# Attention result turned on the vector engine and moved by 64-byte transfers, in a fused attention and mixture-of-experts kernel

## The reference

```python
# attention: H = 8 heads, dqk = 2, dv = 16
q = (x @ Wq.T + bq).reshape(B, M, H, dqk)
k = (x @ Wk.T + bk).reshape(B, M, H, dqk)
v = (x @ Wv.T + bv).reshape(B, M, H, dv)
scores = einsum('bmhd,bnhd->bhmn', q, k) / sqrt(dqk)
scores = where(scores >= 0, scores, 0.2 * scores)
beta = softmax(scores, axis=-1)
out = einsum('bhmn,bnhd->bmhd', beta, v).reshape(B, M, C)
return gamma * out + x
...
# experts: router, top 2 of 16 experts (12 with two layers of 512), a capacity for each, weighted sum
h = gelu(einsum('ech,efh->ecf', dm, fc1_weight) + fc1_bias)
out_mlp = einsum('ecf,ehf->ech', h, fc2_weight) + fc2_bias
...
x = x + attention(xn) + experts(xn)
```

## Time and profile before

| | us |
|---|---|
| median of 3 runs | 977.33 (976.41 to 978.05) |
| the profiled execution | 976.61 |
| its span in the trace | 974.8 |
| PE busy, of the span | 883.5 (91%) |
| DVE busy | 744.3 (76%) |
| ACT busy | 716.5 (74%) |
| POOL busy | 581.7 (60%) |
| DMA queue of SP and the transfers of ACT, share of 16 engines | 14.8% and 0.3% |

### The profile page before, as it was taken

The page is one execution under the profiler, slowest core; times in us unless marked ns, Lnnn a source line. Parts: engine busy times, 40 slices in busy tenths (PEclk is TensorE's granted clock), DMA queues, the critical chain, the costliest instruction groups (busy, mean ns, idle before and its releaser), DMA issues.

```text
span 974.8 us, 19803 instructions
## 1 busy us (share of the span) xinstructions
PE 883.5 (91%) x7619; PEld 365.8 (38%) x7620; DVE 744.3 (76%) x851; ACT 716.5 (74%) x859; POOL 581.7 (60%) x574
## 2 busy tenths in 40 slices
PE   0688249999999999999999989999999999999997
PEld 0444102333333333867767723333333333333332
DVE  6698889999999995001011089999999999999996
ACT  0689878888888887454454468888888888888886
POOL 3355137776676662999999015647566574665770
PEclk9999659999999999999999989999999999999999
DMA  8723100101100011242342210010011002002100
GB/s 228 269 65 72 31 27 30 44 30 36 39 25 28 18 52 58 68 135 92 110 135 78 80 43 26 22 49 20 26 32 39 23 21 64 24 13 62 31 7 22
DMA packets 48163, 55.34 MB, mean 57 GB/s; under 512 B 10714, under 2 KB 35122, under 8 KB 48080
## 3 DMA queue, kind: packets, MB, share of 16 engines
q1 hardware_dynamic: 38464, 44.10, 14.8%
q0 software_dynamic: 8192, 9.37, 3.3%
q10 hardware_dynamic: 1424, 0.76, 0.3%
HBM read 31.58 MB, written 30.02 MB: 63 GB/s over the span
## 4 chain that ended last, share of the span: by engine, by line
PE 77%; ACT 9%; DVE 6%; issue 4%; DMA 1%; SPq 1%; POOLq 0%; ACTq 0%; DVEq 0%
PE ps L765 26%; PE ps L745 15%; PE ps L735 13%; PE ps L825 8%; PE ps L817 8%; ACT pr L636 4%; PE ps L775 3%; ACT ot L628 2%; DVE xn L897 1%; SPq L248 1%; PE ps L695 1%; PE ps L806 1%; ACT y L614 1%; DMA y<-in_x 1%; ACT va L592 1%
## 5 line engine op out<-in xcount | busy, mean ns | idle before, releaser
L1030 DVE TENSOR_SCALAR ps<-ps 128x1024 f32<-128x1024 f32 x512 | 610.7, 1229 | 20.9 <-PE ps L735 6.6
L636 ACT ACTIVATE pr<-ps 128x1024 f32<-128x1024 f32 x512 | 523.3, 1024 | 111.5 <-PE ps L745 101.0
L765 PE MATMUL ps<-pr,vp 128*32 128x256 f32 x4096 | 327.7, 392 | 0.3
L745 PE MATMUL ps<-q,kz 64*128 64x512 bf16 x1024 | 201.7, 391 | 9.2 <-DVE ps L1030 9.1
L735 PE MATMUL ps<-q,kz 62*128 62x512 bf16 x1024 | 199.9, 387 | 7.7 <-DMA q<-parts_dram 1.7
L445 POOL DMA_INDIRECT xs<-eout,idxs x128 | 129.0, 1008 | 108.7 <-ACT pr L636 78.5
L430 POOL DMA_INDIRECT disp<-xn,idx x128 | 125.6, 981 | 47.1 <-issue 35.8
L1042 DVE TENSOR_TENSOR pr<-ps,parts 128x1024 f32<-128x1024 f32 x12 | 14.7, 1225 | 166.1 <-PE ps L825 166.1
L745 PEld LDWEIGHTS ps<-q,kz 64*128 64x128 bf16 x1024 | 49.2, 93 | 222.0 <-DVE ps L1030 117.2
L765 PEld LDWEIGHTS ps<-pr,vp 128*32 128x32 f32 x4096 | 81.2, 108 | 108.1 <-issue 91.3
L663 ACT ACTIVATE pr<-ps,b1s 128x512 f32<-128x512 f32 x96 | 66.0, 687 | 48.8 <-PE ps L817 48.8
(11 more groups left out here) (120 smaller groups left out, 618.6 us busy)
## 6 DMA issues: line engine op xcount, KB each, us to landing
disp<-pr SPq DMA_DIRECT2D x12, 512.0 KB, 4.9
eout<-pr SPq DMA_DIRECT2D x12, 512.0 KB, 2.9
y<-in_x SPq DMA_DIRECT2D x8, 512.0 KB, 8.2
out<-y SPq DMA_DIRECT2D x8, 512.0 KB
w<-in_w1t SPq DMA_DIRECT2D x12, 256.0 KB, 3.1
w<-in_w2t SPq DMA_DIRECT2D x12, 256.0 KB, 3.3
xs<-disp SPq DMA_DIRECT2D x6, 512.0 KB, 4.8
pr<-disp SPq DMA_DIRECT2D x6, 512.0 KB, 4.8
```

Of the source, the lines that this page charges most:

```text
L636: act.activation(pr[:, c % BUFS, 2 * pair:2 * pair + 2, :], ring[i % RING], ACT.Exp, scale=SLOPE).then_inc(S["exps"], 1)
L745: last = pe.matmul(ring[i % RING][:, k, :], kz[r:r + TILE, hg, pair, kc * P:(kc + 1) * P], q2[r:r + TILE, hg, qh * HALF:(qh + 1) * HALF], ...
L765: last = pe.matmul(acc[p % 2][32 * g:32 * g + 32, cols], vp[:, hg, kc, g, :], pr[:, c % BUFS, g % PAIRS * 2 + g // PAIRS, cols], start=(kc ...
L1030: dve.tensor_scalar(s, s, 0.0, 1.0 / SLOPE - 1.0, ALU.max, ALU.mult).then_inc(S["relu"], 1)
```

## The change

DVE turns `acc` by one transpose of 32x32 blocks, which is read from PSUM and written to `ot` in SBUF, at unit 5 of the next pass. After it, row q of the 32-row block g of `ot` holds the 16 results and the denominator of one token and head; DVE takes the reciprocals at unit 6, now from `ot`. POOL multiplies (`quotient`) into `att`. Tokens sit on the wrong partitions then: 16 transfers on SP's queue (`spread`), each of 32 partitions by 4 pieces of 16 elements (64 bytes), bring them to `moved`, and POOL adds `moved` to `y` as before. ACT's copy and PE's four transposes are gone. `spread(p)` is issued two passes later in SP's queue, and `operands_in` places the operand loads between spreads at the same points of the passes as before. POOL does the quotient of pass p-1 and the addition of pass p-2 behind its transfers of pass p.

```diff
+TURN = 5
+PARTS = 1
+BLOCK = 32
...
+            def spread(p):
+
+                sp.wait_ge(S["att_rdy"], p + 1)
+                wait_done(sp, "y_att", p - 1)
+                for g in range(HG):
+                    rows = att[BLOCK * g:BLOCK * g + BLOCK, p % 2, :, :].rearrange("q (t r) d -> q t r d", r=P // BLOCK)
+                    for r in range(P // BLOCK):
+                        sp.dma_start(moved[BLOCK * r:BLOCK * r + BLOCK, p % 2, :, g, :], rows[:, :, r, :]
+                                     ).then_inc(S[f"spread{p % 2}"], 16)
...
+            for p in range(BH * NPB):
+                operands_in(p)
+                if p > 1:
+                    spread(p - 2)
             sp.wait_ge(S["scat"], 16 * GS)
...
             sp.wait_ge(S["pv"], BH * NPB * TB)
+            spread(BH * NPB - 2)
             load_expert(1, 1)
+            spread(BH * NPB - 1)
...
+            spread(B * NPB - 1)
+            store_sequence(B - 1)
...
+            def quotient(p):
+
+                pool.wait_ge(S["rg_rdy"], p + 1)
+                wait_done(pool, f"spread{p % 2}", 16 * HG * GT * (p // 2))
+                rows = ot[:, p % 2, :].rearrange("p (q c) -> p q c", c=BLOCK)
+                pool.tensor_tensor(att[:, p % 2, :, :], rows[:, :, 0:DV],
+                                   rg[:, p % 2, :].unsqueeze(2).broadcast_to([P, HALF // BLOCK, DV]), ALU.mult
+                                   ).then_inc(S["att_rdy"], 1)
...
                     if p > b0 * NPB:
-                        settle(p - 1)
+                        quotient(p - 1)
+                    if p > b0 * NPB + 1:
+                        settle(p - 2)
+                quotient(b1 * NPB - 1)
+                settle(b1 * NPB - 2)
                 settle(b1 * NPB - 1)
...
-                    if i % UP == EVAC and i > first + UP:
-                        evacuate(i // UP - 1)
...
-                    wait_done(pe, "att_rdy", p - 1)
+                    wait_done(pe, "turned", p - 1)
...
-                    if 0 <= i % UP - TURN < GT and i > first + UP:
-                        turn(i // UP - 1, i % UP - TURN)
...
+            def turn(p, part):
+
+                if part == 0:
+                    dve.wait_ge(S["pv"], TB * (p + 1))
+                    wait_done(dve, "att_rdy", p - 1)
+                cols = slice(part * HALF // PARTS, (part + 1) * HALF // PARTS)
+                last = dve.transpose(ot[:, p % 2, cols], acc[p % 2][:, cols])
+                if part == PARTS - 1:
+                    last.then_inc(S["turned"], 1)
```

More of the change, by code:

```diff
@@ L199, in build @@
                  "qz_init weighted gate_rdy row_step route max_rdy off_rdy reset_rdy r_exp cnt_rdy pos_rdy ztile init_rdy kz_init "
-                 "ld0 ld1 vp_rdy s1 relu s2 exps pv acc_evac o_rdy rg_rdy att_rdy y_att "
+                 "ld0 ld1 vp_rdy s1 relu s2 exps pv turned rg_rdy att_rdy spread0 spread1 y_att "
                  "scat staged pool_step carry "
@@ L309, in store_sequence, with operands_in @@
                              y[:, bass.ts(s, TB), :]).then_inc(S["final"], 16)
[L312 to L315, removed]
+            def spread(p):
[6 more added lines that the diff above has]
+                                     ).then_inc(S[f"spread{p % 2}"], 16)
+            def operands_in(p):
+                if p % NPB == 0 and p > 0:
+                    load_operands(p // NPB, 1)
+                if p % NPB == NQ and p // NPB + 1 < B:
+                    load_operands(p // NPB + 1, 0)
+            for hg in range(NHG):
+                load_operands(0, hg)
+            for p in range(BH * NPB):
+                operands_in(p)
+                if p > 1:
+                    spread(p - 2)
             sp.wait_ge(S["scat"], 16 * GS)
@@ L341, in _ @@
                 store_expert(E_MLP - 2 + u)
[L343 to L349, removed]
+            for p in range(BH * NPB, B * NPB):
+                operands_in(p)
+                if p > BH * NPB + 1:
+                    spread(p - 2)
+                if p % NPB == 0 and p > BH * NPB:
+                    for s in STORES[p // NPB - BH - 1]:
+                        store_sequence(s)
+            spread(B * NPB - 2)
+            for s in STORES[B - BH - 1][:-1]:
                 store_sequence(s)
+            spread(B * NPB - 1)
+            store_sequence(B - 1)
             sp.wait_ge(S["final"], 16 * B)
@@ L492, in settle @@
                 if p >= BH * NPB:
-                    done = share(p + 1, BH * NPB, B * NPB, NG)
+                    done = share(p + 2, BH * NPB, B * NPB, NG)
                     pool.wait_ge(S["comb"], CO0 + (NG if done.stop == NG else max(done.stop - 1, 0)))
@@ L770, in values @@
                     last.then_inc(S["pv"], 1)
[L772 to L777, removed]
             def attention(b0, b1):
@@ L792, in attention @@
                     values(j // PAIRS, j % PAIRS)
-                for t in range(GT):
-                    turn(end // UP - 1, t)
             attention(0, BH)
@@ L1022, in attention @@
                 for i in range(first, end):
-                    done = i // UP - 1 if i > first + UP else None
-                    if done is not None and i % UP == DENOM:
-                        denominators(done)
-                    if done is not None and i % UP == FINISH:
-                        finish(done)
+                    if 0 <= i % UP - TURN < PARTS and i > first + UP:
+                        turn(i // UP - 1, i % UP - TURN)
+                    if i % UP == TURN + PARTS and i > first + UP:
+                        denominators(i // UP - 1)
                     dve.wait_ge(S["s1"], i + 1)
@@ L1030, in attention @@
                     dve.tensor_scalar(s, s, 0.0, 1.0 / SLOPE - 1.0, ALU.max, ALU.mult).then_inc(S["relu"], 1)
+                for part in range(PARTS):
+                    turn(end // UP - 1, part)
                 denominators(end // UP - 1)
-                finish(end // UP - 1)
             attention(0, BH)
```

40 lines of the change are left out of this document (13 added, 27 removed).

## The result

The changed kernel takes **983.26 us** (median of 5 runs, 981.41 to 984.88), the kernel before 977.33. The ratio is 1.0058 (95% interval 1.0043 to 1.0074). I had said 967.0 and a range up to 982.5. The profiled execution took 983.26 us with a span of 981.4, against a span of 974.8 before.

A forecast was written before the change was run, and what follows sets the result against it. It took a loop of PE and ACT to bound attention, with DVE close behind. 974.8 - 24.3 + 8.7 - 1.0 + 6.8 = 965.0 us of span, so 967.0 us; own range 964 to 971, whole range 961 to 982.5.

The forecast's parts named there:

- What bounds the kernel: Attention passes: a loop of PE and ACT sets plain units of 1.20 us; transposes and copy add 0.81 us a pass.
- The DVE turn: Attention passes: DVE's transpose and reciprocal make relus late beyond a room of 0.37 us; stall 0.29 us a pass, +8.7 us.
- The base of 19.22: Attention passes: 20.03 us less the 0.81 us that transposes and copy give back, before DVE's stall is added.
- the one on SP: SP's queue: each of the 16 added transfers takes 0.33 us to issue, 5.3 us a pass, hidden inside the stages.
- At the end: After the last pass: transpose, reciprocal, quotient, 16 issues, landing and addition sum to 9.75 us against 2.94 before, +6.8 us.
- Between the stages: Experts' turn: PE starts 1.4 us earlier, expert 1's load behind a spread costs +0.4 (0 to 7); net -1.0 us.
- Dear transfers, slower: Rival on SP's queue: each of the 16 transfers takes 0.77 us, end and experts lose, 983 us; chance 11%.
- Half-rate transpose: Rival in the attention passes: DVE's transpose slot is 1.13 us, stall 0.80 us a pass, 982.6 us; chance 12%.
- The gain goes back inside the pass: Rival in the passes: DVE late in every unit or POOL's quotient late, 972 to 982 us; chance 15%.
- The turn hides wholly: Rival in the passes: slot 0.57 and room 0.44 us, stall near 0.15 us a pass, 963 us; chance 10%.
- the signs that I listed as wrong: Transpose over 0.9 us, reciprocals 20 apart, issues over 0.5, PE waiting over 2 for expert 1, POOL waiting for spreads inside stages.
- The bound of 7.7 us a pass: DMA engines: a spread's 2048 packets at 60 ns take at most 7.7 us of each engine a pass, hidden.

The follow-up runs named there:

- the probe: The kernel before with 32 idle transfers of eight kinds, in fours, on SP's queue in the second attention stage; 976.82 us in its one execution.
- the split: The changed kernel with DVE's transpose in two halves at units 5 and 9 and the reciprocal moved to unit 13; 978.91 us, ratio 1.0017.

## Why the prediction was wrong

**What bounds the kernel** was right: a plain unit of 1.20 us, transposes and copy worth 0.81 us a pass. **The DVE turn** was right in mechanism and a little dear: stall 19.42 - 19.22 = 0.20 us a pass, not 0.29. The mechanism stands by three points: the whole piece once costs 0.20, in halves almost nothing, twice 0.61 more. The waits at the two units came as forecast, 0.74 - 0.57 = 0.17 and 0.73 - 0.57 = 0.16 where I had 0.18 each; what was off is the time given back behind them, some 0.13 us and not 0.07. The base of 19.22 is my sum's and no run shows it: my 1.207 us a relu would make 19.31 for 16 of them, and the nearest measured pass is the 19.26 of the halves. The attention stages came to -18.4 us where the terms gave -24.3 + 8.7 = -15.6.

**The step that failed** is the one on SP: "I take 0.33, near the loads, with 0.32 and 0.77 as ends". The kind of transfer decides an issue's price, and I took the value of another kind. The loads run from DRAM to SBUF; the spreads run from SBUF to SBUF, as only `kz<-rowones` did, at 0.77 in the mean. I set that row aside as "queued behind other work", which no row showed. One issue of the eight was long (1.62); the other seven took 0.65 each, and the probe shows 0.62 to 0.68. This one term, at 0.64 from start to start, makes all of the error that matters:

- At the end the forecast was +6.8 and it was +17.6. The 16 issues took 10.7 us instead of 5.3, and 6.05 us were added by the spreads of two earlier passes still in the queue. The prediction put this wait at nothing: I had looked only at what waits for POOL's late quotient on DVE, and not at SP, whose next spreads are bunched by it.
- Between the stages I wrote that the room of 6.7 us was used up, and took +0.4 with 0 and 7 as ends. It was +6.9: the load left 5.4 us later than at 0.33. The other 0.93 + 0.55 = 1.5 us are PE's at the granted clock of 0.50 behind its wait, for which I had no term.

In sum: 965.0 - 2.8 (passes) + 0.2 (between the stages) + 6.5 (experts) + 10.8 (end) + 1.7 (prologue) = 981.4 us of span. The 1.7 us before the first relu are no term of the change that I can name: the nine further kernels that carry it have the same prologue and start their first relu at 136.57 to 138.17, on both sides of the 137.17 of before; the profiled run of the changed kernel was the latest.

**The rivals.** "Dear transfers, slower" was what happened: it said 983, with its threshold at about 0.6 us an issue. It priced the end at +13.4 and had not the queueing of 6 us, but put more on the experts (6.7 and 3) than the 6.9 that they cost. So its 983 is close partly by luck: a term that it lacked and terms that it had too high offset each other. I gave it 11% when the one row of its kind spoke for it. "Half-rate transpose" fell with the row of 0.71 us. "The gain goes back inside the pass" fell with passes of 19.42. "The turn hides wholly" is nearly the truth for the stages and needs the split to be all of it. Of the signs that I listed as wrong, two came: issues over 0.5 us, and PE waiting for expert 1 by more than 2 us. The third, POOL waiting for spreads, came only in the last pass of a stage and behind it (41.9 us in four waits), not inside.

**Packets.** The bound of 7.7 us a pass on their time held with room to spare. The Trainium skill that I had weighed ("DMA: Bandwidth & Descriptors", Specifications and Rules for kernel authors) says two things: transfers under 512 bytes are below line rate, and many small ones should be joined. These runs bear out the second: one transfer in place of 16 gave 960.27 us, though with the tokens misplaced. The size of the pieces alone changed nothing here (64 bytes 983.26, 256 bytes 982.86).

## What to carry to other kernels

Price an added transfer by the issuing queue's time for its own kind (which memories it runs between) times the number of instructions; bytes and packets came second here. If the nearest row of the right kind looks disturbed, take it apart issue by issue before you turn to a clean row of another kind. Then look at the two places where a queue's time is not hidden: where a stage ends, and where the queue holds a load that another engine wants next. Reordering such a queue helps only if what is moved back has room. And a step put between an engine's units is free up to the room that each unit has, so cut it into pieces smaller than that and set them apart.

## What was not expected of the hardware

- From SBUF to SBUF, SP's issue time in a row of issues hardly depended on the shape: 0.62 to 0.68 us for 2 partitions and for 128, for 64-byte and 256-byte pieces, and 0.65 for the single rows of `kz<-rowones`. With DRAM on one side it did: 0.43 in 256-byte rows, 0.64 in 64-byte pieces to DRAM, 0.25 to 0.32 for the operand loads from DRAM. Why is open.
- Writing to DRAM and reading back (2.9 + 2.2 us) beat the direct way in SBUF with its 16 issues (10.7 + 1.4 us).
- The packets that the change adds, most of them of 64 bytes, took about 10 ns of a DMA engine each.
- DVE turned 128x512 f32 from PSUM to SBUF in 32x32 blocks in 0.71 us, with the next relu 0.63 after its start.
